# One-hot rows of four small tables in two VectorE comparisons instead of one (DLRM tower, one core)

## What is computed

```python
e = jnp.stack([tbl_0[ids[:, 0]], ..., tbl_49[ids[:, 49]]], axis=1)   # 2048 x 50 x 16
gram = jnp.einsum('bid,bjd->bij', e, e)
z = gram[:, _I_IDX, _J_IDX]                                        # pairs i < j
h = jnp.concatenate([z, dense_ctx], axis=1)
h = jnp.maximum(h @ W_top1 + b_top1, 0.0)                          # 512
h = jnp.maximum(h @ W_top2 + b_top2, 0.0)                          # 256
y = h @ W_top3
```

## Time and profile before

| | |
|---|---|
| time, median of 3 executions | 452.78 us (452.11 to 453.46) |
| time of the profiled execution | 453.39 us |
| its span, first to last instruction | 451.3 us |
| mean granted TensorE clock | 0.890 of 2.4 GHz |
| busy: PE, DVE, ACT, POOL | 342.9, 295.8, 198.8, 322.7 us |

### The profile page before, as it was taken

One profiled execution on the slowest core, in us unless ns is written; L12 is line 12 of the kernel. 1 busy time (PEld: TensorE's weight loads), 2 busy tenths in 40 slices (PEclk: granted clock), 3 DMA queues, 4 the chain that ended last, 5 costly groups with the idle time before them and its releaser, 6 DMA issues.

```text
span 451.3 us, 13158 instructions
## 1 busy us (share of the span) xinstructions
PE 342.9 (76%) x5633; PEld 247.4 (55%) x5633; DVE 295.8 (66%) x606; ACT 198.8 (44%) x288; POOL 322.7 (71%) x318
## 2 busy tenths in 40 slices
PE   0568167566488979979989699798895948989886
PEld 0567067565366657666666476656653525454543
DVE  2599899999357579758576687566715437165551
ACT  2335712246235774455457653445487324140511
POOL 5788777777777777787777777778777777776020
PEclk9978659978679997989999969699998895988999
DMA  6994503423321344243213433111121222212020
GB/s 161 407 367 142 173 7 101 118 77 86 82 44 39 104 115 94 63 136 88 47 32 103 115 95 65 36 43 36 40 53 24 66 50 50 48 15 61 5 61 1
DMA packets 24638, 38.92 MB, mean 86 GB/s; under 512 B 8532, under 2 KB 15876, under 8 KB 24452
## 3 DMA queue, kind: packets, MB, share of 16 engines
q1 hardware_dynamic: 14166, 35.04, 24.0%
q0 software_dynamic: 9920, 2.55, 6.6%
q10 hardware_dynamic: 494, 0.49, 0.3%
HBM read 26.98 MB, written 0.14 MB: 60 GB/s over the span
## 4 chain that ended last, share of the span: by engine, by line
PE 34%; DVE 18%; ACT 13%; SPq 11%; issue 10%; DMA 8%; POOL 5%; another core or an unknown queue 0%; DVEq 0%; ACTq 0%; POOLq 0%
PE hid_ps L881 12%; SPq L383 11%; DVE onehot L490 9%; PE look_ps L803 8%; ACT gram L1010 6%; POOL emb L448 5%; DMA ids_bc<-ids_dram 5%; PE mid_ps L938 5%; PE gram_ps L820 3%; ACT z_both L1077 2%; DVE turned L604 2%; PE gram_ps L841 2%; ACT looked L1047 2%; DMA z_both<-gram 2%; DVE w_sb L672 1%
## 5 line engine op out<-in xcount | busy, mean ns | idle before, releaser
L448 POOL DMA_INDIRECT emb<-tbl,gidx x304 | 318.9, 1049 | 95.7 <-issue 88.4
L881 PE MATMUL hid_ps<-w_sb,z_both 127*128 127x512 f16 x462 | 112.3, 386 | 0.0
L803 PE MATMUL look_ps<-parts,onehot 125*128 125x64 f16 x1836 | 75.0, 203 | 44.5 <-DVE onehot L490 29.9
L490 DVE TENSOR_SCALAR onehot<-ids_bc,rows 125x2048 f16<-125x2048 f16 (+1 forms) x144 | 92.2, 690 | 19.2 <-PE look_ps L803 14.7
L803 PEld LDWEIGHTS look_ps<-parts,onehot 125*128 125x128 f16 x1836 | 69.5, 105 | 56.2 <-issue 20.8
L1010 ACT ACTIVATE gram<-gram_ps 50x784 f32<-50x784 f32 x96 | 78.2, 815 | 29.6 <-PE gram_ps L820 26.7
L803 PE MATMUL look_ps<-parts_med,onehot 125*128 125x128 f16 x800 | 57.1, 233 | 14.4 <-DVE onehot L490 13.8
L881 PEld LDWEIGHTS hid_ps<-w_sb,z_both 127*128 127x128 f16 x462 | 41.5, 99 | 46.1 <-issue 3.3
L803 PEld LDWEIGHTS look_ps<-parts_med,onehot 125*128 125x128 f16 x800 | 53.1, 105 | 20.6 <-DVE parts_med L663 13.9
L490 DVE TENSOR_SCALAR onehot<-ids_bc,rows_med 125x1024 f16<-125x1024 f16 x100 | 45.8, 495 | 28.2 <-PE look_ps L803 24.4
L1047 ACT ACTIVATE looked<-look_ps 128x1024 f16<-128x1024 f32 (+1 forms) x28 | 26.7, 954 | 67.0 <-PE look_ps L803 66.6
(11 more groups left out here) (74 smaller groups left out, 221.7 us busy)
## 6 DMA issues: line engine op xcount, KB each, us to landing
ids_bc<-ids_dram SPq DMA_DIRECT2D x28, 512.0 KB
emb<-tbl,gidx POOLq DMA_INDIRECT x304
z_both<-gram SPq DMA_DIRECT2D x31, 121.0 KB
z_both<-w SPq DMA_DIRECT2D x1, 2816.0 KB
z_both<-gram SPq DMA_DIRECT2D x31, 90.8 KB
z_both<-gram SPq DMA_DIRECT2D x152, 6.2 KB
z_both<-gram SPq DMA_DIRECT2D x31, 60.5 KB
gram<-small SPq DMA_DIRECT2D x2, 512.0 KB, 5.1
```

What stands on the lines that cost most here:

```text
L448: pool.indirect_dma_start(emb[:, T % TPC, f, :], None, big[f], bass.IndirectOffsetOnAxis(ap=gidx[:, T, f:f + 1], axis=0)).then_inc(landed, 16)
L490: nc.vector.tensor_scalar(onehot[0:TP, s % RING, 0:cnt, :], ids_bc[0:TP, o % IDS_BUFS, 0:cnt, :], row, None, ALU.is_equal).then_inc(onehot ...
L803: last = nc.tensor.matmul(bank[:, half, at:at + width], onehot[0:TP, at_ring, i, t * TILE:(t + 1) * TILE], moving.rearrange("p i s d -> p ...
L881: return nc.tensor.matmul(hid_ps[:, :], z_parts[0:KP, T % 2, x, k, :], w1_sb[0:KP, k, w, :], start=(i == 0), stop=(i == L1_MM - 1))
```

## The change

A slice of four tables is compared by two instructions of two tables (1024 elements) each. Only the second one signals `onehot_ready`. Slices of two tables or one are compared by one instruction as before.

```diff
+COMPARED = 2
...
-                nc.vector.tensor_scalar(onehot[0:TP, s % RING, 0:cnt, :], ids_bc[0:TP, o % IDS_BUFS, 0:cnt, :],
-                                        row, None, ALU.is_equal).then_inc(onehot_ready, 1)
+                for i in range(0, cnt, COMPARED):
+                    tables = slice(i, min(i + COMPARED, cnt))
+                    last = nc.vector.tensor_scalar(onehot[0:TP, s % RING, tables, :], ids_bc[0:TP, o % IDS_BUFS, tables, :],
+                                                   row, None, ALU.is_equal)
+                last.then_inc(onehot_ready, 1)
```

## The result

| | median | executions | ratio to before (95% interval) |
|---|---|---|---|
| before, beside the first runs of the change | 453.12 us | 4 | |
| the change | 464.33 us | 4 | 1.0243 (1.0174 to 1.0312) |
| the change once more (another chip) | 466.37 us | 6 | 1.0269 (1.0225 to 1.0314) |

The change makes the kernel 11 to 12 us slower, where 6.2 were forecast (459.0, range 455.0 to 463.8): the sign is right, the size about half of what came.

A forecast was written before the change was run, and what follows sets the result against it. DVE's start phase and slot 0 were taken to bound the kernel up to 90.5 us, POOL alone from there to 367. 453.39 + 0.2 + 1.95 + 2.1 + 2 = 459.6 us profiled, median 459.0, range 455.0 to 463.8.

The forecast's parts named there:

- the gate: POOL's first wait for pair products, before the gather at 90.54 us; claimed to tie the end to DVE's transpose until then.
- the term of 4.2 us for the gate: DVE's added time in start phase and slot 0 delays POOL's first wait for pair products, opening at 90.27 + 4.2.
- The price of a slice: On DVE, two 1024-element comparisons take 0.79 us instead of 0.66 for one of 2048: +0.13 us each slice.
- The start phase and slot 0: DVE's work ahead of tile 0's transpose: +2.15 us in the start phase, +2.1 us for 16 comparisons in slot 0.
- I take half, +2 us: Gathers after the gate lose more beside halves: +3.9 us over 19 groups, halved to +2; bounds -10.4 and +9.5.
- the second, full loss: Gathers after the gate suffer fully beside halves: 453.39 + 4.2 + 9.5, median 466.5; chance 0.11 (462 to 467).
- Rival 3: At the first wait for pair products: no gate, or second half nearly free; 452.8 to 454; no change, chance 0.06.
- Rival 1: Short comparisons let gathers in sooner beside full groups after the gate: up to -6.2 us, 446.6 us; chance 0.05.
- Rival 4: DVE becomes the bound in slots 4, 5, 8 and 9: 14.3 us less 9.7 of slack is 4.6; no chance given.
- DVE's wait in slot 12: Sign: in slot 12 DVE still waits 6 to 10 us for `emb`, tile 12's gathered rows; before, 9.70 us.
- G: The prediction's theory: DVE's added time reaches the end through the first wait for pair products, where POOL waits 3 us or more.
- Theory B: Formed during the experiments: beside comparisons a gather's 1.25 us cycle stretches to a whole number of distances between comparison starts.

The follow-up runs named there:

- chunks 2 and 3 alone: Halves only in chunks 2 and 3 (62 of 124 slices), whole comparisons elsewhere, against the kernel before: ratio 1.0070 (1.0041 to 1.0098).
- the quarters: Each comparison covers one table (512 elements), the medium group's slices divided too, against the kernel before: ratio 1.0793 (1.0751 to 1.0835).
- three and one: Slices of four tables compared by two instructions of three and one tables (1536 and 512 elements), against the kernel before: ratio 1.0165 (1.0123 to 1.0207).

## Why the prediction had the sign right and the size wrong

- **What bounds the kernel.** POOL alone after the gate: shown (chunks 2 and 3 alone cost 3.2 us, though DVE still waits 10.31 us in slot 12 there). "Up to 90.5 us the end is set by whatever makes `turn(0)` late": this is the step that failed. It was true of the kernel before, with 0.77 us between the two chains. I priced the change on one of them, DVE's, and let POOL's 61 gathers ahead of the gate cost nothing, though their loss beside comparisons was the subject of the next paragraph. They lost 8.1 us, more than DVE's 5.0, and the gate opened unnoticed. So the term of 4.2 us for the gate failed as a path: the stretch up to the gate cost 7.3 us, on POOL's chain.
- **The price of a slice,** 0.13 us: right. The start phase and slot 0 together: 4.2 forecast, the transpose 5.0 late. One by one the two terms are not confirmed: with halves in chunk 0 alone the transpose is 1.2 us late (2.15 forecast), with halves in chunk 1 alone 1.4 (2.1 forecast), in single profiles that differ by 1 us where the code is the same.
- **After the gate.** The term "I take half, +2 us" was mis-sized: 6.0 measured. The account by the rows of the run at 60 us (1.55 to 1.58) gave 3.9 and its upper bound 9.5. The halving had no row behind it; beside halves some gathers miss one chance more than that run shows, and a few miss a whole run of comparisons (4.27 us). The kernel before had such gathers too (3.03 us at the most), only fewer.
- **The sum.** 4.2 + 2 were to be 7.3 + 6.0. Of the rivals the second, full loss, came nearest (466.5, at 0.11), for its time; its gate term is wrong in the same way, so its nearness is luck in part. Rival 3 said that the gate would be no gate, which came true, but by another cause: it took DVE's added time to be covered, while here POOL was later still. Its time (452.8 to 454) was far off.
- **Rival 1** (short comparisons let gathers in) failed at 1024 elements and came mostly true at 512, where it costs DVE the time instead. The Trainium skill's "SBUF — State Buffer", section "Who interferes with whom", says that whoever issues first gets the shared ports for the whole instruction and the other blocks; the quarters show both directions in one profile: comparisons of 0.55 us for 0.34 beside gathers of 0.94, and the gather of 6.02. But the comparison lost only 0.2 us, not the gather's whole 0.94, and no run here shows that it is the order of issue that decides.
- **Rival 4** was near: DVE's chain came 11.4 us late to slot 12, between the 6.2 of the text and the 14.3 of the rival, and stayed behind POOL's.
- The signs named ahead: 0.40 us within a slice and DVE's wait in slot 12 came (12.66, above the 6 to 10 named). The gap of 3 us at the gate didn't, and that was the sign to tell G by. DVE's busy time rose by 16 us in the listing and not by 30: the listing counts the overlap of two neighbours once (102.5 us for 248 of a mean 0.480), so it can't be multiplied out from the mean.

Open: why a gather beside halves sometimes takes one chance more (1.68 instead of 1.28) and now and then gets none in a whole run of comparisons. Theory B names the shortest cycle, not this; no run shows what decides it.

## What to carry to other kernels

When a change touches an engine that slows another, price it on every chain up to each meeting point, not only on the one that waits there last: here 0.77 us lay between the two. An instruction's cost to a neighbour that it delays depends on the rhythm, not on its busy time alone: the same 0.79 us of DVE cost 12 us as two halves and 7.5 as three and one. And where the neighbour is the bound and DVE waits anyway, short instructions can give time back.

## What the runs showed of the hardware

Beside fp16 comparisons 0.66, 0.87 and 0.40 us apart, gathers that come every 1.25 us alone mostly came every 1.33, 1.71 to 1.75, and 1.58 to 1.98; single ones lasted for a whole run of comparisons, up to 4.27 us. Beside 512-element ones, 0.26 us apart, nearly all ran at or near their free 0.94 us (one took 6.02), and it was the comparison that took 0.55 instead of 0.34. I had expected neither the beat nor that the loser mostly changes with the size.
